# One attention pipeline around the expert stage, and the value products ahead of the logits in a slot

## The chip, the cores and the metric

The kernel runs on one core of a Trainium2 chip. The time is that of one launch on the device, in microseconds (us). All arithmetic is float32, or float32r: a float32 rounded so that TensorE takes it in one pass, and a product that must be exact is three such passes over a high and a low part.

## The reference, cut to what matters

```python
x  = L0_attn_X                      # 32 sequences x 256 rows x 128
xn = layernorm(x)
# attention: 16 heads of 64; position bias from 10 basis functions per head
Q, K, V = xn@Wq + bq, xn@Wk, xn@Wv
R = xn@Wr + br                      # 10 numbers per head and row
logits = Q K^T / 8 + causal mask + sum_n R[t, n] * b_nd[n, t - p]   (0 <= t - p < 128)
A = softmax(logits) V @ Wproj + bproj
# mixture of 8 experts, 128 -> 512 -> 128, two per row, weights softmaxed
top, idx = top_k(xn @ router_w.T, 2)
F = sum_k softmax(top)[k] * (gelu(xn w1[idx_k] + b1) w2[idx_k] + b2)
out = x + A + F
```

## The kernel before, in words

Every engine runs one list of instructions in order, written out by hand; semaphores tie the lists together. After a preparation (norm, weights split into two parts, router and the place of every row) come three stages.

**Attention of sequences 0 to 15.** A sequence has four quads of heads (a quad is two pairs, a pair two heads), and each engine takes one *slot* per quad (`sequence`, TensorE's at L1494). A slot `d` of TensorE holds, in this order: `keys` (L1430, queries and keys of the next quad's first pair), a *unit* at place 0, `logits` of quad d (L1450), `values` of quad d-2 (L1463, probabilities times values), units at place 1, `turn_probs` (L1439, transposed probabilities of quad d-1, first pair), `keys` of the next quad's second pair, units at place 2, `outputs` of quad d-2 (L1483, projection), units at place 3, `turn_probs` of the second pair. A unit is a product for the values ("v"), for R ("r", of the next sequence) or for the position bias ("g"); the table `UNITS` (L355) says in which slot and place it stands and whether it belongs to the next sequence. All units use one PSUM bank, so each waits until ScalarE has copied the one before (`unit_taken`). A "g" unit ("g", half t) reads `rT`, which SyncE fills by six transfers in `spread_weights` (L499) from the rounded R; its result goes to `gst`, by DMA to `skew` in HBM and back into `extra`, shifted along the diagonal.

ScalarE's slot (L852) is: copy of the value unit, copy of the first keys into `qk` (it waits until the logits that read that half of `qk` are done), exponentials of quad d's first pair, first tile (`exponentials`, two of 128x128, L839), copy of `headT` (`heads_out`, L845: what `values` made), copy of the unit at place 1, exponentials of the first pair's second tile, unit at place 2, second keys, unit at place 3, four exponentials of the second pair.

VectorE's slot (L1161) is: inverses; `bias_sums` of the first pair (L1136: it merges the two halves of the logits, adds the bias and takes the minimum, L1143 and L1149); `copy_probs` (L1125); `bias_sums` of the second pair; `copy_probs`; `add_heads` of quad d-2 (L1184, L1191), which frees the bank that `values` and `outputs` share; in the third stage `add_rows` adds the experts' rows. `values` waits for `add_heads` of the quad before. GpSimd scales the probabilities (`norms`) and moves rows by indirect DMA.

**Experts.** The rows of each expert lie in 39 blocks of 512. TensorE's `experts` (L1386) transposes block b+1 (`turn_x`), makes block b's hidden layer and block b-1's output. Before this stage the attention pipeline is emptied: two more slots hold values, transposes and outputs of sequence 15 alone. On four engines the middle of the stage is a loop.

**Attention of sequences 16 to 31** starts from nothing: SyncE spreads R of sequence 16, the first five "g" units follow each other, then slot 0. At the end the pipeline is emptied again.

The tiles of the experts and of attention overlap in SBUF.

## Time and profile before

| | |
|---|---|
| median of 3 runs | 1521.05 us (1520.63 to 1524.2) |
| the profiled execution, whole | 1505.93 us |
| its span, first to last instruction | 1503.8 us |
| TensorE busy (matmul) | 1341.1 us, 89% |
| ScalarE busy | 996.9 us, 66% |
| VectorE busy | 836.5 us, 56% |
| GpSimd busy | 765.9 us, 51% |
| mean granted TensorE clock | 0.959 |

The profile is of one execution, whose whole time is 15.1 us below the median. A row of a timeline gives its start in us from the span's beginning, its length, engine, source line, operation, what it writes and reads, and in brackets how long the engine was idle before it and what ended that. Matmuls overlap: the time that one takes on the engine is the distance to the next start. Two attention stages of about 525 and 535 us stand around an expert stage of about 266 us.

### The profile page before, as it was taken

What the parts mean: (1) busy time and instruction counts of PE and PEld (TensorE: products, weight loads), DVE (VectorE), ACT (ScalarE), POOL (GpSimd) and SP (SyncE); (2) the same over time, 40 slices, a digit from 0 to 9 for tenths busy, and PEclk for the clock granted to TensorE, in tenths of its full rate; (3) what the DMA queues carried; (4) which work ended last, traced back from release to release, by engine and by line L of the source; (5) the groups of instructions that cost most, each with busy time, mean ns of one, the idle gap of its engine ahead of it and who ended that gap; (6) DMA issues with size and microseconds to landing.
All of it is one profiled execution on the core that took longest, in us unless ns stands there. A gap on an engine that the chain in (4) does not pass through costs nothing.

```text
span 1503.8 us, 36197 instructions
## 1 busy us (share of the span) xinstructions
PE 1341.1 (89%) x10631; PEld 1118.1 (74%) x10631; DVE 836.5 (56%) x3523; ACT 996.9 (66%) x3088; POOL 765.9 (51%) x1518
## 2 busy tenths in 40 slices
PE   2472899999999999989999999599999999999997
PEld 1131688788878788868999999477887877778885
DVE  4675466666666666662222121156676666667766
ACT  1131688788888788865454544277888877788885
POOL 0340567777766777760000000177776666777764
PEclk8795899999999999999999999699999999999999
DMA  9775577777777677755666665476776777777773
GB/s 288 265 245 194 159 206 211 196 208 202 201 198 217 197 210 201 201 169 161 206 199 204 200 205 183 119 195 195 205 215 194 198 193 195 203 203 212 196 201 92
DMA packets 458681, 298.62 MB, mean 199 GB/s; under 512 B 20586, under 2 KB 432788, under 8 KB 458516
## 3 DMA queue, kind: packets, MB, share of 16 engines
q1 hardware_dynamic: 450324, 279.86, 64.4%
q0 software_dynamic: 8192, 16.79, 3.9%
q8 instruction: 75, 1.23, 0.3%
q14 instruction: 90, 0.74, 0.2%
HBM read 135.01 MB, written 145.77 MB: 187 GB/s over the span
## 4 chain that ended last, share of the span: by engine, by line
PE 69%; SPq 13%; DMA 8%; DVE 3%; issue 3%; ACT 2%; POOL 1%; DVEq 0%; POOLq 0%; ACTq 0%
PE ps L1459 10%; PE ps L1382 9%; PE ps L1478 9%; SPq L507 8%; PE ps L1346 8%; PE ps L1348 7%; PE ps L1347 7%; PE ps L1446 6%; PE ps L1488 5%; PE ps L1415 5%; DMA rT<-r_lo 5%; DMA skew<-gst 2%; ACT gst L814 1%; PE ps L1364 1%; SPq L482 1%
## 5 line engine op out<-in xcount | busy, mean ns | idle before, releaser
L839 ACT ACTIVATE prob<-logit,low 128x128 f32<-128x128 f32 x1024 | 402.1, 398 | 19.2 <-DVE low L1149 5.6
L1149 DVE CUSTOM_DVE_ANT_0 logit<-ps,extra 128x128 f32<-128x128 f32 x1024 | 256.1, 288 | 125.7 <-PE ps L1459 116.5
L1131 DVE TENSOR_TENSOR probT<-ps,keep 128x512 f32<-128x512 f32 x256 | 177.1, 692 | 240.0 <-PE ps L1446 240.0
L713 POOL TENSOR_SCALAR prob<-prob,inv 128x128 f32<-128x128 f32 x512 | 186.7, 365 | 153.2 <-DVE inv L1159 151.8
L669 POOL CAST r_hi<-r_raw 80x512 fp32r<-80x512 f32 x32 | 19.4, 607 | 411.3 <-ACT r_raw L808 411.3
L814 ACT COPY gst<-ps 128x512 f32<-128x512 f32 x256 | 150.9, 590 | 114.0 <-PE ps L1415 102.2
L1459 PEld LDWEIGHTS ps<-qk 64*128 64x128 f32 x2048 | 169.7, 190 | 61.3 <-issue 48.9
L1459 PE MATMUL ps<-qk 64*128 64x256 f32 (+1 forms) x2048 | 206.7, 342 | 0.0
L1478 PE MATMUL ps<-probT,val 128*64 128x256 f32 (+1 forms) x2048 | 194.7, 332 | 7.0 <-DVE acc L1191 7.0
L839 ACT ACTIVATION_READ_ACCUMULATOR prob<-logit,low 128x1 f32 x1024 | 196.5, 192 | 0.0
L1415 PE MATMUL ps<-basis,rT 120*128 120x512 f32 x256 | 129.2, 505 | 69.1 <-DMA rT<-r_lo 59.8
L715 POOL TENSOR_SCALAR prob<-prob,inv 128x128 f32<-128x128 f32 x512 | 185.5, 362 | 0.0
L1478 PEld LDWEIGHTS ps<-probT,val 128*64 128x64 f32 x2048 | 127.4, 136 | 59.2 <-issue 4.3
L829 ACT COPY qk<-ps 128x512 f32<-128x512 f32 x256 | 149.4, 583 | 32.2 <-PE ps L1459 26.1
L1346 PE MATMUL ps<-xq_hi,wqk_hi 128*128 128x256 f32 x512 | 167.0, 326 | 2.7 <-ACT qk L829 2.7
L1446 PE MATMUL ps<-ident,prob 128*128 128x128 f32 x1024 | 154.7, 273 | 4.3 <-POOL prob L715 3.6
L681 POOL DMA_INDIRECT x_place<-xrow,at_now x128 | 129.0, 1008 | 41.9 <-issue 28.3
L1382 PEld LDWEIGHTS ps<-w2b,hid 128*128 128x128 f32 x1248 | 145.2, 192 | 3.3
L1348 PE MATMUL ps<-xq_hi,wqk_lo 128*128 128x256 f32 x512 | 146.6, 286 | 0.0
L1347 PE MATMUL ps<-xq_lo,wqk_hi 128*128 128x256 f32 x512 | 146.2, 286 | 0.0
L1382 PE MATMUL ps<-w2b,hid 128*128 128x128 f32 x1248 | 145.4, 275 | 0.0
L683 POOL DMA_INDIRECT yget<-y_place,at_now x128 | 128.3, 1003 | 31.7 <-issue 27.3
(176 smaller groups left out, 2475.6 us busy)
## 6 DMA issues: line engine op xcount, KB each, us to landing
skew<-gst SPq DMA_DIRECT2D x384, 256.0 KB
extra<-skew SPq DMA_DIRECT2D x256, 256.0 KB, 3.8
w1b<-w_d SPq DMA_DIRECT2D x39, 514.0 KB, 3.6
w2b<-w_d SPq DMA_DIRECT2D x39, 320.0 KB, 3.4
rT<-r_hi SPq DMA_DIRECT2D x128, 80.0 KB
x_place<-zero SPq DMA_DIRECT2D x39, 256.0 KB, 2.8
placed<-x_place SPq DMA_DIRECT2D x39, 256.0 KB, 3.8
y_place<-yrow SPq DMA_DIRECT2D x39, 256.0 KB, 2.3
```

The source lines that it names most:

```text
L713: nc.gpsimd.tensor_scalar(prob[:, h, 0:P], prob[:, h, 0:P], inv[:, h, 0:1], 1.0, ALU.mult, ALU.mult).then_inc(norm_made, 1)
L715: nc.gpsimd.tensor_scalar(prob[:, h, P:], prob[:, h, P:], inv[:, h, 1:2], 1.0, ALU.mult, ALU.mult).then_inc(norm_made, 1)
L839: ins = nc.scalar.activation(prob[:, h % PB, cols], logit[:, h % LB, cols], ACT.Exp, scale=-1.0, bias=low[:, h % LB, t:t + 1], accum_out=t ...
L1149: ins = nc.vector.tensor_tensor_reduce(out=logit[:, h % LB, cols], in0=ps[:, b + n, cols], in1=extra[:, h, cols], scale=1.0, scalar=BIG, o ...
L1346: nc.tensor.matmul(dst, a_hi, b_hi, start=start, stop=False)
L1347: nc.tensor.matmul(dst, a_hi, b_lo, start=False, stop=False)
L1348: return nc.tensor.matmul(dst, a_lo, b_hi, start=False, stop=stop)
L1382: mm = nc.tensor.matmul(ps[:, Y_BANK[u], t * P:(t + 1) * P], hid[:, u, c, t * P:(t + 1) * P], w2b[:, u, c * P:(c + 1) * P], start=(c == 0) ...
L1415: mm = nc.tensor.matmul(ps[:, MISC_BANK, :], rT[:, par, n // 2, n % 2, tile * P:(tile + 1) * P], basis[:, :], start=True, stop=True)
L1446: mm = nc.tensor.transpose(ps[:, PT_BANK, a:a + P], prob[:, (2 * pair + n) % PB, k * P:(k + 1) * P], ident[:, :])
L1459: mm = nc.tensor.matmul(ps[:, S_BANK[pair % 2][n], cols], qk[rows, pair % 2, 0, q], qk[rows, pair % 2, 1, k], start=True, stop=True)
L1478: mm = nc.tensor.matmul(ps[DQ * n:DQ * n + DQ, HEAD_BANK, q], val[:, s, v:v + DQ], probT[:, hh % 4, p], start=(s == 0), stop=(s == 1), ski ...
```

## The change

- TensorE: in a slot `values(i, d - 2)` stands ahead of `logits(i, d)`. No other engine's slot is reordered.
- `UNITS`: the next sequence's first "g" unit moves from the end of slot 1 to place 1 of slot 2, the second to place 3 of slot 2, the third and fourth to places 1 and 2 of slot 3. Slot 1 has one "g" unit fewer, slot 3 one more.
- One pipeline over all 32 sequences. The expert stage stands inside it, in front of slot 0 of sequence 16: values and outputs of quads 2 and 3 of sequence 15 come after the experts, and the "g" units and keys of sequence 16 before them. Each engine waits for what its half-done work needs.
- The experts' loops are written out. SyncE fetches the experts' first weights and rows during sequence 15.
- SyncE: a bias transfer back is issued after the next write or two of the same sequence, and no longer carried over to the next.
- SBUF is laid out anew so that what lives across the expert stage (`extra`, `val`, `probT`, `qk`, `prob` and others) does not overlap it; `rT` is two tiles.

The hunks are, in order: the table, SyncE's order, ScalarE's, VectorE's, TensorE's slot and TensorE's list.

```diff
-        UNITS = [(0, 0, "v", 0, 0, 0), (0, 1, "g", 2, 1, 0), (0, 2, "r", 0, 0, 1), (0, 3, "g", 3, 0, 0),
-                 (1, 0, "v", 0, 1, 0), (1, 1, "g", 3, 1, 0), (1, 3, "g", 0, 0, 1),
-                 (2, 0, "v", 1, 0, 0), (2, 1, "g", 0, 1, 1), (2, 3, "g", 1, 0, 1),
-                 (3, 0, "v", 1, 1, 0), (3, 1, "g", 1, 1, 1), (3, 3, "g", 2, 0, 1)]
+                 (1, 0, "v", 0, 1, 0), (1, 1, "g", 3, 1, 0),
+                 (2, 0, "v", 1, 0, 0), (2, 1, "g", 0, 0, 1), (2, 3, "g", 0, 1, 1),
+                 (3, 0, "v", 1, 1, 0), (3, 1, "g", 1, 0, 1), (3, 2, "g", 1, 1, 1), (3, 3, "g", 2, 0, 1)]
...
             def sequence(i, more=True):
-                positions(i, POSITIONS_OWN[:2])
+                write_unit(i, *POSITIONS_OWN[0])
+                write_unit(i, *POSITIONS_OWN[1])
+                read_unit(i, *POSITIONS_OWN[0])
                 if more:
                     spread_weights(i + 1)
+                read_unit(i, *POSITIONS_OWN[1])
+                positions(i, POSITIONS_OWN[2:])
                 if i >= HALF + 2:
                     store(i - HALF - 2)
-                positions(i, POSITIONS_OWN[2:])
                 if more:
-                    positions(i + 1, POSITIONS_AHEAD)
+                    positions(i + 1, POSITIONS_AHEAD[:2])
+                    if i == HALF - 1:
+                        first_rows()
+                    positions(i + 1, POSITIONS_AHEAD[2:])
...
+            for i in range(B):
+                if i == HALF:
+                    for t in range(2):
+                        act.wait_ge(skew_out[t], (HALF * GROUPS + 3 - t) * 16 * (t + 1))
                     high_part(0, 0)
-                    for b in range(3):
+                    for b in range(PLACES):
                         experts(b, b % 2, b // 2)
...
+            for i in range(B):
+                if i == HALF:
+                    dve.wait_ge(prob_made, HALF * PAIRS)
                     low_x(0, 0)
...
                     if heads:
                         units(i, d, 0, more)
-                        logits(i, d)
                     if here(i, d - 2, heads, start):
                         values(i, d - 2)
+                    if heads:
+                        logits(i, d)
...
+            for i in range(B):
+                if i == HALF:
+                    unit_taken(pe, *START[-1], HALF)
                     turn_x(0, 0, 0)
+                    pe.wait_ge(logit_made, HALF * PAIRS)
+                    pe.wait_ge(pT_made, HALF * PAIRS - 2)
+                    pe.wait_ge(key_made, HALF * PAIRS + 2)
+                    for b in range(PLACES):
                         experts(b, b % 2, b // 2, b % ROWS_AHEAD, b // ROWS_AHEAD)
                     expert_out(PLACES - 1, (PLACES - 1) % 2, (PLACES - 1) // 2)
+                    pe.wait_ge(y_made, PLACES)
+                sequence(i, 0, more=i + 1 < B)
+            sequence(B, 0, heads=False, more=False)
```

## Rows read from the trace of the kernel before

**Rows 1.** Waits of TensorE, 300 to 660 us: total us, times, longest
```profile
PE ps L1415 <- DMA rT<-r_lo: 13.2, 11, 1.6
```

**Rows 2.** Timeline of TensorE: start us, us, operation; one slot, and the next slot's logits
```profile
1028.40 1.58 PE L1459 MATMUL ps<-qk 64*128 64x256 f32 x16
...
1029.91 1.52 PE L1478 MATMUL ps<-probT,val 128*64 128x256 f32 x16
...
1031.36 0.50 PE L1415 MATMUL ps<-basis,rT 120*128 120x512 f32 x1
...
1032.84 1.05 PE L1488 MATMUL ps<-wproj,headT 128*128 128x128 f32 x8
...
1033.65 0.48 PE L1415 MATMUL ps<-basis,rT 120*128 120x512 f32 x1
...
1033.97 0.60 PE L1446 MATMUL ps<-ident,prob 128*128 128x128 f32 x4
...
1034.32 0.36 PE L1346 MATMUL ps<-xq_hi,wqk_hi 128*128 128x256 f32 x1
...
1035.12 0.39 PE L1346 MATMUL ps<-wv_hi,xq_hi 128*128 128x512 f32 x1
...
1035.92 1.58 PE L1459 MATMUL ps<-qk 64*128 64x256 f32 x16
```

**Rows 3.** Timeline of ScalarE in the same slot
```profile
1029.42 0.59 ACT L829 COPY qk<-ps 128x512 f32<-128x512 f32 x1 [0.18 <-PE ps L1459]
1030.39 0.40 ACT L839 ACTIVATE prob<-logit,low 128x128 f32<-128x128 f32 x1 [0.38 <-DVE low L1149]
1030.79 0.39 ACT L839 ACTIVATE prob<-logit,low 128x128 f32<-128x128 f32 x1
1031.47 0.59 ACT L849 COPY headT<-ps 128x512 f32<-128x512 f32 x1 [0.20 <-PE ps L1478]
1031.96 0.59 ACT L814 COPY gst<-ps 128x512 f32<-128x512 f32 x1
...
1033.22 0.58 ACT L829 COPY qk<-ps 128x512 f32<-128x512 f32 x1
```

**Rows 4.** Timeline, the emptying of the pipeline after sequence 15
```profile
672.34 0.63 PE L1446 MATMUL ps<-ident,prob 128*128 128x128 f32 x4
...
674.51 1.52 PE L1478 MATMUL ps<-probT,val 128*64 128x256 f32 x16 [1.54 <-DVE acc L1191]
676.07 0.59 ACT L849 COPY headT<-ps 128x512 f32<-128x512 f32 x1 [4.96 <-PE ps L1478]
676.71 1.16 PE L1488 MATMUL ps<-wproj,headT 128*128 128x128 f32 x8 [0.68 <-ACT headT L849]
```

**Rows 5.** Timeline of TensorE: logits of slots 0 and 1, a "g" unit
```profile
1003.82 1.58 PE L1459 MATMUL ps<-qk 64*128 64x256 f32 x16
...
1012.09 1.58 PE L1459 MATMUL ps<-qk 64*128 64x256 f32 x16
...
1018.62 0.47 PE L1415 MATMUL ps<-basis,rT 120*128 120x512 f32 x1 [1.03 <-DMA rT<-r_lo]
```

**Rows 6.** Timeline of TensorE: first and last logits of each attention stage, expert products
```profile
153.22 2.93 PE L1459 MATMUL ps<-qk 64*128 64x256 f32 x16
...
661.56 1.58 PE L1459 MATMUL ps<-qk 64*128 64x256 f32 x16
...
679.79 0.47 PE L1346 MATMUL ps<-xb_hi,w1b 128*128 128x512 f32 x1 [0.76 <-DVE xb_lo L1216]
...
936.65 7.30 PE L1382 MATMUL ps<-w2b,hid 128*128 128x128 f32 x64
...
969.47 2.93 PE L1459 MATMUL ps<-qk 64*128 64x256 f32 x16
...
1481.27 1.58 PE L1459 MATMUL ps<-qk 64*128 64x256 f32 x16
```

**Rows 7.** Windows: length, busy (instructions) by engine, TensorE clock, DMA share, GB/s
```profile
663.00:680.00 17.00, 11.86 (x101) 8.89 (x98) 8.57 (x32) 6.34 (x21) 7.05 (x19) 1.00 0.47 144
```

More of the change, by code:

```diff
@@ L482, in read_unit @@
                 sp.dma_start(dst, src).then_inc(skew_in[2 * g + t], 16)
-            written = []
             def positions(i, units):
-                for g, t in units:
-                    wait_from(sp, skew_in[2 * g + t], i * 16)
+                for n, (g, t) in enumerate(units):
                     write_unit(i, g, t)
-                    if written:
-                        read_unit(*written.pop())
-                    written.append((i, g, t))
-            def positions_end():
-                read_unit(*written.pop())
+                    if n > 0:
+                        read_unit(i, *units[n - 1])
+                read_unit(i, *units[-1])
             def spread_weights(seq):
@@ L544, in _ @@
             fetch_rows(0)
-            for i in range(HALF):
-                sequence(i, i + 1 < HALF)
             def first_weights(b, u, k):
@@ L583, in experts, with first_rows @@
                     block_out(b - 1, 1 - u, None)
-            sp.wait_ge(logit_made, HALF * PAIRS)
-            first_weights(0, 0, 0)
-            second_weights(0, 0, 0)
-            sp.wait_ge(spread, TILES * TOP * 16)
-            for b in range(3):
-                block_rows(b, b)
-            for b in range(BLOCKS_FIRST):
-                experts(b, b % 2, b % ROWS_AHEAD)
-            with sp.Fori(0, BLOCK_TURNS) as m:
-                for r in range(ROWS_AHEAD):
-                    b, u, _ = block_of(m, r)
-                    experts(b, u, (BLOCKS_FIRST + r) % ROWS_AHEAD)
-            for b in range(BLOCKS_FIRST + ROWS_AHEAD * BLOCK_TURNS, PLACES):
+            def first_rows():
+                first_weights(0, 0, 0)
+                second_weights(0, 0, 0)
+                sp.wait_ge(spread, TILES * TOP * 16)
+                for b in range(3):
+                    block_rows(b, b)
+            for i in range(HALF):
+                sequence(i)
+            for b in range(PLACES):
                 experts(b, b % 2, b % ROWS_AHEAD)
             block_out(PLACES - 1, (PLACES - 1) % 2, None)
-            spread_weights(HALF)
-            positions(HALF, POSITIONS_AHEAD)
             for i in range(HALF, B):
@@ L705, in moves_of @@
             def moves_of(i, way, d, more):
-                moves = MOVES_FINAL if way is FORTH and not more else MOVES
+                moves = MOVES_FINAL if i == HALF - 1 else MOVES
                 return [n for n, at_d in enumerate(moves) if at_d == d]
@@ L741, in _ @@
             pool.wait_ge(xnT_made, 1)
-            for s0, way in ((0, FORTH), (HALF, BACK)):
-                s1 = s0 + HALF
-                if way is BACK:
-                    pool.wait_ge(s_psum, HALF * PAIRS)
-                split_q(s0, 0)
-                round_weights(s0)
-                if way is FORTH:
-                    pool.wait_ge(w_stored, 32)
-                    pool.wait_ge(zeroed, PLACES * 16)
-                    pool.wait_ge(route, 2)
-                sequence(s0, 0, way, s0)
-                for i in range(s0 + 1, s1 - 1):
-                    sequence(i, i % 2, way, s0)
-                sequence(s1 - 1, 1, way, s0, more=False)
-                sequence(s1, 0, way, s0, heads=False, more=False)
+            split_q(0, 0)
+            round_weights(0)
+            pool.wait_ge(w_stored, 32)
+            pool.wait_ge(zeroed, PLACES * 16)
+            pool.wait_ge(route, 2)
+            for i in range(B):
+                sequence(i, i % 2, FORTH if i < HALF else BACK, 0, more=i + 1 < B)
+            sequence(B, 0, BACK, 0, heads=False, more=False)
         @block.scalar
@@ L894, in high_part @@
                 nc.scalar.copy(xb_hi[:, u, :], ps[:, XB_BANK[u], :]).then_inc(xb_high, 1)
[L896 to L907 removed]
+            for n, (kind, k, t) in enumerate(START):
+                unit(n, kind, k, t, 0)
+            keys(0, 0)
+            keys(0, 1)
+            for i in range(B):
+                if i == HALF:
+                    for t in range(2):
+                        act.wait_ge(skew_out[t], (HALF * GROUPS + 3 - t) * 16 * (t + 1))
                     high_part(0, 0)
[L909 removed]
+                    for b in range(PLACES):
                         experts(b, b % 2, b // 2)
[L911 to L915 removed]
+                sequence(i, 0, more=i + 1 < B)
+            sequence(B, 0, heads=False, more=False)
         @block.vector
@@ L1232, in experts @@
                     block_y(b - 1, 1 - u, k if u == 1 else k - 1)
[L1234 to L1248 removed]
+            for i in range(B):
+                if i == HALF:
+                    dve.wait_ge(prob_made, HALF * PAIRS)
+                    low_x(0, 0)
+                    for b in range(PLACES):
                         experts(b, b % 2, b // 2)
                     block_y(PLACES - 1, (PLACES - 1) % 2, (PLACES - 1) // 2)
+                sequence(i, 0, more=i + 1 < B)
+            sequence(B, 0, heads=False, more=False)
             for d in range(2 * TOP):
```

132 lines of the change are left out of this document (37 added, 95 removed).

## The prediction

> **What bounds the kernel now.** First the table of engines: TensorE is busy 89% of the span and no other engine above 66%. Then TensorE's waits in the middle of the first attention stage: in 360 us it waited for one thing worth naming, the landing of `rT`, 13.2 us in 11 times [rows 1], one per sequence. Then one slot in the timeline: from logits at 1028.40 to the next logits at 1035.92 the starts follow each other without a gap, so a slot of two "g" units is 7.52 us of pure TensorE work [rows 2]. ScalarE in the same slot has small waits (0.18, 0.38, 0.20) and stays ahead [rows 3]. A sequence is 1035.92 - 1003.82 = 32.10 us: slot 0 (with the "r" unit) 8.27, slots 2 and 3 7.52 each, which leaves 8.79 for slot 1, 1.03 of it the wait for `rT` [rows 2, 5]. Last, the ends of the stages: between the last logits of sequence 15 and the first of 16 lie 307.9 us, of which the expert products hold 943.95 - 679.79 = 264.2 [rows 6]; emptying and filling cost the other 43.7.
>
> **The wait for `rT` goes.** The first "g" unit that reads the new `rT` stood at the end of slot 1, and stands after place 0 of slot 2 now. It was 1.03 us too early [rows 5] and comes some 4 us later, so nothing is late in its place. Slot 1 also loses one unit, 0.32 us (1033.65 to 1033.97, [rows 2]), and slot 3 gains it. If nothing else changed, the slots would be 8.27, 7.2, 7.52 and 7.84: 30.85 per sequence.
>
> **One pipeline.** TensorE enters the experts after the second transposes of slot 3. Behind it ScalarE still has its last exponentials and the wait for `skew` writes, queued ahead of the first cast of expert rows, and VectorE the subtraction behind that. I take 5 us from transposes to first product (at least 2, if only the cast and the subtraction are left; at most 8, if the last write's landing shows in full). Then 264.2 of expert products, unchanged (weights and rows were fetched ahead there too), and 1.9, an estimate (at least 1, at most 4), for the last block's result, which TensorE now waits for before it goes on, and for ScalarE's change back to the exponential in slot 0. Insertion: 271 us, in place of 307.9 less one slot.
>
> **Values ahead of logits.** This is the part that decides. Let S be the start of `values` in a slot. Values take 1.45 (1029.91 to 1031.36), so the logits start at S+1.45, and the unit at place 1 at S+2.95 as before; from there TensorE's list is the old one and reaches the outputs at S+4.44 (1032.84 - 1028.40) [rows 2]. ScalarE's order is unchanged, and everything in it from the copy of `qk` on hangs on the logits. Before, the first exponential started 1.99 after the logits (1030.39 - 1028.40), released by VectorE, whose list is likewise bound to them; `headT`, behind two exponentials, could start 0.79 later (0.40, 0.39) but waited for the values until 3.07 [rows 3]. Now: first exponential S+1.45+1.99 = S+3.44, `headT` S+4.23 to 4.82, and the outputs, 0.05 behind its end (676.66 to 676.71, [rows 4]), S+4.87 in place of 4.44. ScalarE goes on: the unit's copy at S+4.72 (0.49 behind), two exponentials, second `qk` at S+5.98 (1.26 behind), done at 6.56 [rows 3]. TensorE: outputs 0.81, unit 0.32, transposes 0.35, so keys could start at S+6.35, but their bank is free at S+6.61. Keys and the value unit take 1.60 (1034.32 to 1035.92, [rows 2]): the next S is at S+8.21, not 7.52.
>
> A second chain comes to nearly the same point. `values` waits for `add_heads` of the quad before, which stands behind both `copy_probs`; emptying the pipeline shows it alone: transposes 672.34, values 674.51, 2.17 later [rows 4]. TensorE's own way is 1.95 (1033.97 to 1035.92), and the logits used to hide the rest. This alone costs 0.22 per slot, and in slots where ScalarE binds it is covered.
>
> Slot by slot. Slot 2: 8.21. Slot 1: one unit less, but `qk` binds: 8.2. Slot 3, three units: the one at place 2 waits for the copy of the first (S+4.72+0.59+0.05 = 5.36, where TensorE is at S+4.44); then unit 0.32, outputs 0.81, the third unit waits for the second's copy, which takes the place of `qk` at S+5.98, until 6.62; unit, transposes, keys and value unit 0.32+0.35+1.60 give 8.9, the second chain 6.94+2.17 = 9.1, the write of `gst` that must have landed about as much: 9.2. Slot 0: the same with the "r" unit, 0.4 longer: transposes at S+7.24, plus 2.17 = 9.4. A sequence: 9.4+8.2+8.2+9.2 = 35.0 us, 4.15 above 30.85. Its bounds: 31.7 if only the second chain costs (four times 0.22), 36.5 if each slot also loses the 0.38 that ScalarE spends waiting for VectorE [rows 3]. I take the schedule, 35.0, since every step of it is a row of the same slot.
>
> **The sum,** first logits (153.22) to last (1481.27), 1328.05 us before [rows 6]. After: sequence 0, whose first slots have no values, 33.7 (7.9+8.4+8.2+9.2); 30 x 35.0 = 1050; insertion 271; sequence 31 up to its last slot, three slots of 8.2, 24.6. Together 1379.3, +51.3; the last logits stand 1.45 later in their slot; what lies before and behind is as it was. 1505.93 + 52.7 = 1558.7 us for the profiled execution. The median of the runs is 15.1 above it, which I add: **1574 us**. Put as gains and losses: some 80 us won by the wait, the restart and smoother sequences, 133 us (32 x 4.15) lost by the new order.
>
> **At no cost.** The written-out loops: the expert products ran with no gap between blocks in the loop, and the attention stages are written out already. SyncE's last reads now wait for their write to land, but no unit is due in those 2 to 3 us; if it were, that wait would come back once per sequence. SyncE's first expert transfers stand in slot 3 of sequence 15 once, beside 4 us in which no write is due. GpSimd has its inverses 0.5 into the slot as before and 2.5 us of room; if the cover went, the transposes would wait.
>
> **A rule that speaks against the change.** With ScalarE's waits TensorE would be busy some 88% of a slot and idle in pieces of 0.2 to 0.9 us. While the pipeline emptied it was busy 11.86 of 17 us, with longer gaps, and the granted clock was 1.00, its 2.4 GHz level [rows 7]. The Trainium skill, "TensorE: Matmul & The Clock Gate" (A second HAM failure mode: psum-queue depth-cycling), says that short idle pieces between groups of matmuls can make the clock oscillate between its two levels; by that rule the time would be the last rival's.
>
> **Rivals.**
> 1. Faster: ScalarE's chain does not bind. Its place is the start of `headT`, its price 4.15 less 0.88 per sequence. For it: ScalarE has idle time in each slot. Against: that idle time is all ahead of `headT`, and the list is in order. Then a sequence is 31.7 and the sum 33+30 x 31.7+271+23.2 = 1278, -50: 1472 us. It decides from a mean slot 0.44 us shorter than mine: at a sequence of 33.2 us the gains and losses meet. 10%.
> 2. In between: a sequence of 33.2, no change, 1521 us. Both chains half covered. 4%.
> 3. The change does not do what it says, in that a wait per sequence remains or comes anew on SyncE's or ScalarE's side (a landing of a write, 1 us each): 36.0 per sequence, 1604 us. 8%.
> 4. Slower still: the clock falls. At the lower level the logits of a slot took 2.93 in place of 1.58 [rows 2, 6]; one slot in ten at 1.9 times its length adds 12.8 x 7 = 90 us: 1660 us. 4%.
>
> **Numbers.** My forecast has 74%, its own range 1555 to 1595 (0.6 us per sequence either way). Below it lie rival 1 and 2 (14%), above it 3 and 4. The range 1540 to 1606 leaves out rival 1, 2 and 4. About 0.3% either way is what this kernel's measurement can tell. Slower 74+8+4 = 86%, less 1 for tails: 0.85; faster 0.12; same 0.03.
>
> **What would show it.** In the profile after: slots of 8.2, 8.2, 9.2 and 9.4 us between starts of values; a wait of TensorE's outputs for ScalarE's `headT` in every slot, 0.4 us; no wait for `rT` in mid-stage; ScalarE's wait for the values before `headT` gone and its wait for the logits before `qk` grown to about 1.4 us; about 271 us added between slot 3 of sequence 15 and slot 0 of 16. I am wrong if the slots stay at 7.5 to 7.7 us, or if TensorE's waits are for VectorE alone.

## The result, and the profile after the change

| | before | after |
|---|---|---|
| median of the runs, us | 1520.84 (1515.09 to 1524.2, 4 runs) | 1607.38 (1604.31 to 1611.28, 4 runs) |
| ratio to before | | 1.0575, 95% interval 1.0534 to 1.0615 |
| profiled execution, us | 1505.93, span 1503.8 | 1611.28, span 1609.5 |
| mean granted TensorE clock | 0.959 | 0.961 |
| first logits to last logits, us | 1328.05 | 1434.87 |

The change made the kernel 5.75% slower. The forecast was 1574 us with a range to 1606: the direction held, the time lies 33 us above the forecast and 1.4 us above the range. The first view is the page's table of engines, after, with the row of TensorE's clock in 40 slices.

```profile
PE 1401.6 (87%) x10631; PEld 1145.8 (71%) x10631; DVE 831.2 (52%) x3523; ACT 979.5 (61%) x3088; POOL 767.2 (48%) x1518
...
PEclk7795999999999999999999999999999999999999
```

TensorE issues as many instructions as before, and its mean clock is the same. Most of the time went into waits. The next view is TensorE's waits in the middle of the first attention stage (300 to 660 us) and then in the second (1035 to 1560 us): total us, times, longest.

```profile
PE ps L1296 <- ACT gst L783: 11.1, 20, 0.8
PE ps L1365 <- ACT gst L783: 3.4, 7, 0.7
...
PE ps L1428 <- DVE acc L1149: 1.1, 2, 0.7
```

```profile
PE ps L1428 <- DVE acc L1149: 35.0, 23, 2.2
PE ps L1365 <- ACT gst L783: 6.6, 14, 0.7
PE ps L1296 <- ACT gst L783: 6.2, 14, 0.5
```

The wait for `rT` of [rows 1] is gone from the middle of the stage. In its place stand waits for ScalarE's copies of units (`gst`), in both stages, and in the second stage alone a large one: the values wait for the additions on VectorE, 35.0 us, up to 2.2 us at a time. A wait names only who came last. The next two timelines show that in both stages part of it begins on TensorE itself, with a signal that comes late.

In its first part a slot of the first half is what the prediction drew up. The timeline of slot 2 of sequence 13, all engines (start, length, operation, idle time before it and who ended it):

```profile
629.15 1.58 PE L1409 MATMUL ps<-qk 64*128 64x256 f32 x16
630.18 0.59 ACT L798 COPY qk<-ps 128x512 f32<-128x512 f32 x1 [1.08 <-PE ps L1409]
630.88 0.40 ACT L808 ACTIVATE prob<-logit,low 128x128 f32<-128x128 f32 x1
...
631.66 0.56 ACT L818 COPY headT<-ps 128x512 f32<-128x512 f32 x1
...
632.28 1.16 PE L1438 MATMUL ps<-wproj,headT 128*128 128x128 f32 x8
...
633.19 0.48 PE L1365 MATMUL ps<-basis,rT 120*128 120x512 f32 x1
...
634.96 0.59 ACT L783 COPY gst<-ps 128x512 f32<-128x512 f32 x1 [1.00 <-PE ps L1365]
...
635.60 0.50 PE L1296 MATMUL ps<-wv_hi,xq_hi 128*128 128x512 f32 x1 [0.61 <-ACT gst L783]
...
637.97 1.58 PE L1409 MATMUL ps<-qk 64*128 64x256 f32 x16
```

In [rows 3] ScalarE waited 0.20 us for the values before `headT`, and 0.18 for the logits before `qk`. Now `headT` finds its values done, and `qk` waits 1.08. The first exponential stands 1.73 us behind the logits, where [rows 3] had 1.99, so `headT` holds the outputs up only a little: they start 0.06 us behind its end. What the prediction did not have comes next. The "g" unit that starts at 633.19 takes 0.48, but ScalarE, idle for 1.00 us, copies it only at 634.96, and the value unit behind that copy starts 0.61 late. The rest of this section shows the same delay at greater length in the second half, and what it goes with.

A slot of the second half looks different. The same view for slot 1 of sequence 17, with GpSimd's indirect moves:

```profile
1044.49 1.58 PE L1409 MATMUL ps<-qk 64*128 64x256 f32 x16
...
1047.08 1.03 POOL L660 DMA_INDIRECT yget<-y_place,at_now  x1 [0.16 <-issue]
...
1048.41 0.95 POOL L660 DMA_INDIRECT yget<-y_place,at_now  x1 [0.30 <-issue]
1048.61 0.60 PE L1396 MATMUL ps<-ident,prob 128*128 128x128 f32 x4
...
1049.67 0.94 POOL L660 DMA_INDIRECT yget<-y_place,at_now  x1 [0.30 <-issue]
...
1051.67 0.69 DVE L1093 TENSOR_TENSOR probT<-ps,keep 128x512 f32<-128x512 f32 x1 [2.37 <-remote]
...
1052.61 0.41 DVE L1149 TENSOR_TENSOR acc<-ps,acc 128x256 f32<-128x256 f32 x1
1053.16 1.87 PE L1428 MATMUL ps<-probT,val 128*64 128x256 f32 x16 [2.15 <-DVE acc L1149]
```

The transposes start at 1048.61 and take 0.60; the copy that waits for them starts at 1051.67. The profile can't name who released it and writes "remote". The records of the semaphores say why: TensorE's increments for the outputs, the transposes, the keys and the value unit, whose modelled ends are 1048.77, 1049.21, 1050.32 and 1051.01, all appear between 1051.55 and 1051.77. In the kernel before, the increments of TensorE in the middle of the attention stages stand within 0.03 us of the instruction's modelled end. After, some records are also missing (117 for 128 outputs, 215 for 256 keys), so the counts below are rough.

Here I call an increment late when its record stands more than 0.5 us behind. Each record is set against the last instruction of its semaphore that had ended, so of two that come in one burst on one semaphore only one is counted. That matters where logits stand first: counted one to one, slot 2 of the first half has 58 for the 44 given below (e1), 60 for 45 (f1), 68 for 54 (f4) and 57 for 40 (g2), and slots 2 and 3 of e1's second half 42 and 26 for 30 and 14. The other counts stay, but for a 13 in place of a 12 in g2. In the middle sequences (1 to 14 and 17 to 30) there are 0 late ones before and 156 after, all in slots 1 and 2, up to 2.8 us. The burst of sequence 13 above is one of them: the "g" unit's increment appears at 634.94, 1.27 us behind its modelled end, and those of the outputs and the transposes within 0.1 us of it. So late signals stand in slots 1 and 2 of both halves; in slot 1 of the first they cost nothing by the table below. Those of ScalarE and VectorE are not late in this kernel: nearly all their records stand within 0.02 us of the instruction's end.

The DMA engines show something at the same instant. Windows of 1 us, columns as in [rows 7]:

```profile
1048.00:1049.00 1.00, 1.00 (x11) 0.97 (x10) 0.97 (x6) 1.00 (x6) 0.70 (x2) 1.00 0.44 96
1049.00:1050.00 1.00, 0.87 (x7) 0.66 (x6) 0.30 (x4) 1.00 (x6) 0.69 (x2) 1.00 0.96 60
1050.00:1051.00 1.00, 1.00 (x6) 0.54 (x4) 0.00 (x0) 0.84 (x5) 0.61 (x1) 1.00 0.81 242
1051.00:1052.00 1.00, 0.01 (x1) 0.00 (x0) 0.33 (x1) 0.21 (x1) 0.00 (x0) 1.00 1.15 346
```

From 1049 to 1050 the DMA engines are taken 0.96 of the time and move only 60 GB/s; two us later they move 346.

TensorE's clock shows it too. The next windows are the slot above from its logits to the end of the wait, and the 3.2 us behind it:

```profile
1044.50:1054.20 9.70, 7.42 (x62) 6.14 (x62) 5.55 (x26) 5.81 (x21) 5.79 (x12) 1.00 0.61 160
1054.30:1057.50 3.20, 3.20 (x22) 2.48 (x18) 0.62 (x5) 0.67 (x2) 3.05 (x8) 0.50 0.32 85
```

Behind the 2.15 us without work the granted clock stands at 0.50, its 1.2 GHz level, for some 3.4 us, and the next logits take 2.85 us for 1.58. This happens in 7 of the 14 sequences 17 to 30, each time behind an idle stretch of 1.9 to 2.2 us in slot 1; but six sequences with as long a stretch keep 1.00. The seven take 38.17 us on average, the six 37.31. In the first half the clock stays at 1.00 throughout.

Means of a slot, from logits to logits, by the timeline of TensorE (first half: sequences 1 to 13, second half: 17 to 29), with the number of late increments by slot:

| kernel | first half: slots 0, 1, 2, 3, sum | second half: slots 0, 1, 2, 3, sum | last logits of 15 to first of 16 | late, first half / second half (slots 0 to 3) |
|---|---|---|---|---|
| before | 8.27 8.92 7.52 7.52, 32.24 | 8.27 9.22 7.63 7.52, 32.64 | 307.9 | none / none |
| forecast | 9.4 8.2 8.2 9.2, 35.0 | the same | 280 | |
| after | 9.14 8.20 8.87 9.05, 35.25 | 9.14 10.42 9.30 8.83, 37.69 | 287.1 | 0 33 40 0 / 0 51 32 0 |

Last, the way into the experts and out of them:

```profile
709.30 1.58 PE L1409 MATMUL ps<-qk 64*128 64x256 f32 x16
...
712.65 1.53 SPq L551 DMA_DIRECT2D placed<-x_place  x3
...
714.29 2.75 SPq L461 DMA_DIRECT2D skew<-gst  x2
...
720.17 0.59 ACT L783 COPY gst<-ps 128x512 f32<-128x512 f32 x1 [5.58 <-DMA skew<-gst]
...
720.81 1.97 PE L1314 MATMUL ps<-ident,placed 128*128 128x128 f32 x8 [5.71 <-ACT gst L783]
...
724.41 1.07 ACT L863 CAST xb_hi<-ps 128x512 fp32r<-128x512 f32 x2 [2.11 <-DMA skew<-gst]
...
725.94 0.76 PE L1296 MATMUL ps<-xb_hi,w1b 128*128 128x512 f32 x1 [3.16 <-DVE xb_lo L1174]
```

```profile
719.80:729.80 10.00, 5.83 (x17) 4.68 (x18) 1.29 (x2) 5.35 (x14) 0.00 (x0) 0.50 0.77 205
```

The first expert product comes some 11 us after the last transposes, where I had taken 5. Behind these waits the granted clock is 0.50 from 719.7 to 729.9, where the kernel before entered the experts at 1.00 (680 to 690 us), and the expert products take 266.65 us for 264.2. At the exit TensorE waits 0.78 us for the last block's result, within the 1.9 that the forecast had for this and ScalarE's change back.

### The profile page after: what moved, and what is told of

Read it like the earlier page. It is cut to its first block, busy times and chain, and to the rows that moved or that the text cites. A ratio compares the mean times of both kernels' runs of the same rounds, so it can differ in the third digit from the quotient of the medians.

```text
span 1609.5 us, 35362 instructions
## 1 busy us (share of the span) xinstructions
PE 1401.6 (87%) x10631; PEld 1145.8 (71%) x10631; DVE 831.2 (52%) x3523; ACT 979.5 (61%) x3088; POOL 767.2 (48%) x1518
## 4 chain that ended last, share of the span: by engine, by line
PE 66%; DVE 9%; issue 8%; ACT 6%; DMA 3%; SPq 3%; another core or an unknown queue 2%; POOL 1%; DVEq 1%; ACTq 0%; POOLq 0%
PE ps L1428 12%; PE ps L1409 9%; PE ps L1332 9%; PE ps L1296 7%; PE ps L1298 6%; PE ps L1297 6%; PE ps L1438 6%; PE ps L1396 5%; PE ps L1365 5%; DVE logit L1111 3%; ACT gst L783 3%; ACT prob L808 3%; DMA skew<-gst 2%; DVE probT L1095 1%
## 5 line engine op out<-in xcount | busy, mean ns | idle before, releaser
L1428 PE MATMUL ps<-probT,val 128*64 128x256 f32 (+1 forms) x2048 | 200.3, 338 | 52.7 <-DVE acc L1149 46.0
L1428 PEld LDWEIGHTS ps<-probT,val 128*64 128x64 f32 x2048 | 142.5, 139 | 130.5 <-ACT val L771 38.4
L1409 PE MATMUL ps<-qk 64*128 64x256 f32 (+1 forms) x2048 | 210.9, 347 | 0.0
L1409 PEld LDWEIGHTS ps<-qk 64*128 64x128 f32 x2048 | 172.9, 194 | 37.2 <-issue 23.9
L1438 PE MATMUL ps<-wproj,headT 128*128 128x128 f32 x1024 | 141.3, 281 | 3.0 <-ACT headT L818 2.3
L1396 PEld LDWEIGHTS ps<-ident,prob 128*128 128x128 f32 x1024 | 126.2, 140 | 23.6 <-POOL prob L692 6.1
```

What stands on the lines that cost most here:

```text
L1396: mm = nc.tensor.transpose(ps[:, PT_BANK, a:a + P], prob[:, (2 * pair + n) % PB, k * P:(k + 1) * P], ident[:, :])
L1409: mm = nc.tensor.matmul(ps[:, S_BANK[pair % 2][n], cols], qk[rows, pair % 2, 0, q], qk[rows, pair % 2, 1, k], start=True, stop=True)
L1428: mm = nc.tensor.matmul(ps[DQ * n:DQ * n + DQ, HEAD_BANK, q], val[:, s, v:v + DQ], probT[:, hh % 4, p], start=(s == 0), stop=(s == 1), ski ...
L1438: mm = nc.tensor.matmul(ps[:, HEAD_BANK, t * E:(t + 1) * E], headT[:, pair, t * P:(t + 1) * P], wproj[:, (2 * quad + pair) % PAIRS, :], st ...
```

## The experiments

The kernel before ran again beside each group of experiments (medians 1522.93 beside e1 to e4, 1518.09 beside f1 to f4, 1521.49 beside g1 to g3), and each ratio is to it. Each experiment is named by its label, e1 to g3. Of the theories that the expectations number, the third is that three or more indirect moves of GpSimd in a row make TensorE's completion signals late; the fourth, that SyncE's reads standing ahead of its own writes do it.

### e1: the order put back in the changed kernel

```
                     units(i, d, 0, more)
+                    logits(i, d)
                 if here(i, d - 2, heads, start):
                     values(i, d - 2)
-                if heads:
-                    logits(i, d)
```

> The change with the slot's order on TensorE undone: logits ahead of values, all else kept. Theory 1 (the new order costs, the rest gains): slots back to 8.3, 7.2, 7.5 and 7.9 us, a sequence 30.9 to 31.2 in both stages, about 1435 us (1425 to 1455). Theory 2 (what made sequences 16 to 31 cost 2.4 us more than 0 to 15 lies in the new SyncE order or unit table and is independent of the order on TensorE): slots 1 and 2 of the second stage stay 0.5 to 2 us above those of the first, 1470 to 1500 us.

Measured: 1484.17 us (1480.92 to 1485.64; a single further run took 3048.71 and stands out of the comparison), ratio 0.9745 [0.9693, 0.9798]. Slots 8.27 7.27 7.68 8.36, 31.57, and 8.27 7.27 8.41 8.83, 32.77; 288.35 between the halves; late 0 17 44 13 / 0 26 30 14. The order alone costs 1607.38 - 1484.17 = 123 us; all the rest of the change gains 38.8. The forecast had 133 and 80. The time lies in the range of theory 2 and not of theory 1, though of theory 2's signs only one came: slot 2 is 0.73 longer in the second half, slot 1 is 7.27 in both. So the costs beside the order are larger than theory 1 had them. Slots 0 and 1 are as drawn up for the old order (8.27 and 7.2), slots 2 and 3 aren't (7.52 and 7.84). In the second half (1000 to 1400 us), ScalarE's waits of this kernel:

```profile
ACT val L771 <- remote: 14.3, 8, 1.8
ACT gst L783 <- DMA skew<-gst: 14.1, 12, 1.8
```

### e2: the new order alone, in the kernel before

The same four lines the other way round in the kernel before.

> The kernel before with one edit: values ahead of logits in TensorE's slot. Theory 1: the two chains behind the new order make slots of 8.2 to 9.4 us here too, while the wait for rT is covered by them: about 35 us per sequence in the first stage, and 37 in the second if what is late there comes with the order; 1610 to 1670 us. Theory 2: 35 us in both stages, about 1605 us, and no late signals of TensorE in slot 1.

Measured: 1614.73 us (1612.21 to 1620.21), ratio 1.0618 [1.057, 1.0666]. Slots 9.14 9.16 9.22 7.97, 35.49, and 9.14 9.97 9.33 7.97, 36.41; 306.95 between the halves; late 0 11 47 0 / 0 17 42 0. So the order costs 1614.73 - 1522.93 = 92 us there, in the range of theory 1. The late increments come with the order alone, without one pipeline: the instruction mix and the moves' order on GpSimd are those of the kernel before, which has none. The order is not needed for them either: e1 has the old one, and 144. Slot 3, with two units, is 7.97, near the 8.2 of the forecast's schedule; with three it is 9.05.

### e3: the moves spread in the changed kernel

```
-        MOVES = (1, 1, 1, 2, 2, 2, 3, 3)
+        MOVES = (0, 0, 1, 1, 2, 2, 3, 3)
```

> The change with GpSimd's eight indirect row moves of a sequence spread as two per slot, in place of none, three, three and two. Theory 3 (TensorE's completions are signalled late in slots 1 and 2 because three indirect moves stand there in a row): slot 1 of the second stage falls from 10.1 to 8.2 us or so and slot 2 in both stages from 8.8 or 9.3 towards 8.2, 25 to 50 us in all, 1555 to 1582 us. Rival (they are late for SyncE's transfers, or moves in slot 0 hurt as much): 1600 to 1620 us.

Measured: 1568.91 us (1561.97 to 1570.33), ratio 1.0295 [1.0247, 1.0343]. Second half 9.14 8.14 7.97 8.89, 34.15: slots 1 and 2 fell from 10.42 and 9.30 to the 8.2 of the forecast, and late increments from 83 to 26. First half 9.14 10.19 7.96 8.88, 36.16: there the transposes of slot 1 wait for the probabilities (26.1 us in 14 times) that GpSimd scales behind the moves, and the moves in slot 0 wait for rows that are fetched only then; in 7 of the 14 sequences the clock falls to its lower level behind that. The values' wait for the additions in the same sequences of the second half is 1.0 us in 3 times, where the changed kernel had 35.0 in 23. The third theory has its first support, and most of the miss is here: 3.54 us a sequence, of which some 0.4 is the clock, which stays at 1.00 in this second half.

### e4: SyncE's write ahead of its reads, in the changed kernel

```
+                write_unit(i, *POSITIONS_OWN[2])
                 read_unit(i, *POSITIONS_OWN[1])
-                positions(i, POSITIONS_OWN[2:])
+                read_unit(i, *POSITIONS_OWN[2])
```

> The change with SyncE's order after the six rT transfers as in the kernel before: the last own unit is written first, then the two transfers back. Theory 4 (the late signals in slot 1 come from a transfer back and the writes issued close behind it): slot 1 of the second stage falls towards 8.2 us, up to 30 us in all, 1575 to 1590 us. Rival: 1600 to 1615 us.

Measured: 1603.76 us (1603.53 to 1607.79), ratio 1.0546 [1.0502, 1.0589]. 35.07 and 37.41 a sequence, late 0 30 41 0 / 0 50 34 0. The fourth theory falls.

### f1: e1 with other moves and the weights fetched earlier

```
+        MOVES_BACK = (0, 0, 1, 1, 2, 2, 3, 3)      # sequences 16 to 31
...
+                if i == HALF - 1:
+                    first_weights(0, 0, 0)
+                    second_weights(0, 0, 0)
                 if more:
                     positions(i + 1, POSITIONS_AHEAD[:2])
```

with the order of e1.

> The changed kernel with three edits: the logits stand ahead of the value products in each slot again (as in e1), in sequences 16 to 31 the eight indirect moves stand as pairs (two in each slot) where they were three in slots 1 and 2, and the first expert's weights are fetched ahead of the last positions before the experts, so that the write of the skewed copy due then isn't behind them. Theory 3 (three indirect moves in a row make TensorE's completion signals late, 1 to 2.8 us in slots 1 and 2): the second half falls from e1's 32.77 us a sequence to about 31.3, 15 times, so 22 to 24 us less; theory of the entry (the write waits behind the weight issues on SyncE): the entry falls from 11 us towards 5, so 5 to 8 us less. Together about 1452 us (1440 to 1465). Rival (the late signals bind only where the value products stand first, and the entry is held by the transfer itself): as e1, 1478 to 1486.

Measured: 1473.23 us (1471.89 to 1476.68), ratio 0.9705 [0.9679, 0.9732], 11 less than e1 and 21 above the expectation. Both parts missed. The stretch between the halves is 288.18, as before the edit: the weights were not what held the write back (the rows' three transfers stood between still). And the second half is 8.66 7.27 7.58 8.73, 32.24: slot 2 gained 0.83, but slot 0 lost 0.39, and 20 late increments turned up in slot 0, where no kernel so far had one. The list offers an explanation: the first move of a slot stands ahead of the normalizing on GpSimd and the others behind it, so two in slot 0 and the first of slot 1 follow each other with only the rounding of R between them, two instructions. I had called them pairs. But e3 has the same list in slot 0 and no late increment there.

### f2: the heads drained earlier on ScalarE

```
                 units(d, 0)
+                if here(i, d - 2, heads, start):
+                    heads_out(i, d - 2)
                 if to_come:
                     keys(*later)
                 if heads:
                     exponentials(i, 2 * d, 0)
-                if here(i, d - 2, heads, start):
-                    heads_out(i, d - 2)
```

in the changed kernel (values first).

> The changed kernel with one move on ScalarE: the heads' outputs are drained ahead of the first copy of the keys and the first exponentials of the slot, not behind them. The theory of chain A (logits, exponentials on ScalarE, the copy of the heads, the outputs on TensorE, about 2 us between logits and outputs that nothing fills) says that slots 0 and 3 shorten by 0.3 to 1.0 each, and the other chain (the additions on VectorE that the value products wait for) takes over: 33.5 to 34.5 us a sequence in the first half in place of 35.2, in all 1555 to 1585. If the chain through the additions already sets every slot, the time stays at 1600 to 1610. If the later exponentials delay the transposes by more than the heads gain: above 1615.

Measured: 1589.58 us (1586.61 to 1594.3), ratio 1.0459 [1.0431, 1.0486]; 5 us above the expectation. Slots 8.66 8.25 8.99 8.62, 34.51, and 8.66 11.32 8.95 8.68, 37.62; late 0 37 54 0 / 0 54 50 0. ScalarE's chain is worth 0.48 us in slot 0, as drawn up, and in slot 3 0.43 in the first half and 0.15 in the second, but slot 1 of the second half loses more than was won. The increments are up to 3.1 us late there, TensorE's idle stretch is 2.3 to 2.8 us, where the changed kernel had mostly 2.0 to 2.2, and behind it the clock falls to its lower level for 3.4 us in all 14 sequences, where it did so in 7.

### f3: f2 with the additions earlier on VectorE

```
+                if here(i, d - 2, heads, start):
+                    add_heads(i, d - 2)
                 if here(i, d - 1, heads, start):
                     copy_probs(i, 2 * (d - 1) + 1)
-                if here(i, d - 2, heads, start):
-                    add_heads(i, d - 2)
```

> f2, and on VectorE the additions stand ahead of the second copy of the transposed exponentials. Both chains of the prediction are shortened. If the two chains are what lengthens a slot with the value products at its head, the slots fall towards the 7.5 to 8.3 of the old order: 32 to 33 us a sequence, in all 1490 to 1540. If VectorE's sum is what counts, the second copy is only late in its turn and the outputs wait for it: 1570 to 1610.

Measured: 1561.22 us (1557.23 to 1568.24), ratio 1.0291 [1.0251, 1.0332]: between the two expectations. Slots 8.47 7.74 8.98 8.49, 33.67, and 8.46 9.56 8.91 8.67, 35.6. Slot 0 has come down to 0.2 of the old order's 8.27. TensorE's waits in the second half (1040 to 1500 us) now name another partner:

```profile
PE ps L1428 <- DVE probT L1095: 15.7, 14, 2.5
```

The values wait for the copy of the second transposes, which is late because the increment of those transposes is: late 0 32 44 0 / 0 46 50 0.

### f4: f1 with the units dealt out evenly

```
-                 (3, 0, "v", 1, 1, 0), (3, 1, "g", 1, 0, 1), (3, 2, "g", 1, 1, 1), (3, 3, "g", 2, 0, 1)]
+                 (3, 0, "v", 1, 1, 0), (3, 1, "g", 1, 0, 1), (3, 3, "g", 1, 1, 1)]
```

and the units of slots 0 to 2 dealt out to match, so that slots 1 to 3 have two "g" units and slot 0 two and the "r" unit; all else as in f1.

> f1 with the units of the fetched keys dealt out so that each slot has two or three short ones and none has the third that waits for the write of the skewed copy to land (slot 3 had three). If that wait (about 1.1 us on TensorE in slot 3 of the changed kernel and of e1) is on the path, 31 sequences lose 0.5 to 1.1 each against f1: 15 to 30 us less, about 1430 to 1440. If the work only moves to another slot, within 5 of f1; if a unit then comes before its read has landed, slower than f1 by 10 or more.

Measured: 1449.89 us (1448.95 to 1451.84), ratio 0.9543 [0.9521, 0.9566], 23 less than f1. The difference is in the expected 15 to 30; the time is 10 above the range that was given with it, since f1 itself came out 21 higher. Slots 8.26 7.52 7.97 7.75, 31.51, and 8.44 7.68 7.71 7.52, 31.35; 283.27 between the halves. In the second half the gain is 0.89 us a sequence (15 of them: 13 us), in the first it is nearly nothing, 0.05: slot 3 is 0.54 shorter, slot 1 has the unit now (7.27 to 7.52), and slot 2 rose from 7.73 to 7.97 with 54 late increments in place of 45. Another 5 us come from the entry to the experts, where in the kernels with three units the third one's copy waits for a write to land (5.58 us in the view above). TensorE's wait for ScalarE's copies in the second half (1000 to 1400 us) is down to one, where e1 had 7.1 us in 11 times:

```profile
PE ps L1298 <- ACT gst L785: 1.1, 1, 1.1
```

### g2: the moves in a row at another place

e1 with

```
+        MOVES_BACK = (0, 0, 0, 1, 2, 3, 3, 3)      # sequences 16 to 31
```

which makes three in a row at the end of slot 0 and, behind the rounding of R, the first of slot 1 as a fourth; none in a row in slots 1 and 2, two in slot 3.

> e1 (logits ahead of the value products) with the eight moves of sequences 16 to 31 as four in a row behind slot 0, one and one, and two at the end. Theory 3 (moves in a row make completion signals late wherever they stand): in the second half slot 0 rises from 8.27 us to 8.8 or more and slot 2 falls from 8.41 to 7.5 or 7.6; the sum about as e1, 32.3 to 33.3 a sequence. Rival (the late signals belong to what else moves in slots 1 and 2, SyncE's writes and reads of the positions): slot 0 stays 8.27 and slot 2 stays above 8.2, or both are clean.

Measured: 1477.47 us (1473.35 to 1480.07), ratio 0.9702 [0.9671, 0.9733]. Second half 8.70 7.74 7.52 8.59, 32.54; late 0 15 40 12 / 45 0 0 6. This is the cleanest answer of the study. The late increments went with the moves: 45 in slot 0, where there were none, and none in slots 1 and 2, where there were 56; slot 0 rose from 8.27 to 8.70 (the theory had 8.8 or more) and slot 2 fell from 8.41 to 7.52, as the third theory said. (Slot 1 rose by 0.47, since the fourth move stands ahead of the normalizing that the transposes wait for.) SyncE's transfers kept their order, with those of slots 1 and 2 still there, so they alone do not make the signals late. In the timeline, slot 0 of sequence 21:

```profile
1113.07 0.95 POOL L661 DMA_INDIRECT yget<-y_place,at_now  x1 [0.30 <-issue]
...
1113.88 0.60 PE L1397 MATMUL ps<-ident,prob 128*128 128x128 f32 x4
...
1114.33 0.95 POOL L661 DMA_INDIRECT yget<-y_place,at_now  x1 [0.30 <-issue]
...
1115.38 0.69 DVE L1094 TENSOR_TENSOR probT<-ps,keep 128x512 f32<-128x512 f32 x1 [1.58 <-PE ps L1397]
```

The transposes' time to the copy is 1.50 us from start to start; in the same kernel three us earlier, with no move beside it, it is 0.64 (1110.84 to 1111.48).

### g1: values first with everything mended

f3 with the units and the weights of f4, and

```
+        MOVES = (1, 1, 2, 2, 3, 3, 3, 3)           # sequences 0 to 15
+        MOVES_BACK = (0, 1, 1, 2, 2, 3, 3, 3)      # sequences 16 to 31
```

so that at most two moves stand in a row, but for three at the end of slot 3 in the first half.

> The value products stay at the head of a slot, and everything that the runs so far name as a cost beside them is mended: heads and additions early (f3), no third unit in slot 3 (f4), and the eight indirect moves so that no more than two stand between two blocks of other work on GpSimd (three in the last slot of sequences 0 to 15). If late completion signals and the unit were what kept f3 above the old order, its 33.7 and 35.6 us a sequence fall to 31.5 to 32.3 and the kernel to 1450 to 1480. If the order itself keeps a price (each slot's value products wait for what VectorE finished last), it stays 1 us a sequence or more above f4, 1490 to 1530.

Measured: 1495.31 us (1493.06 to 1497.52), ratio 0.9833 [0.9802, 0.9864]. Slots 8.47 7.76 7.82 8.94, 32.98, and 8.47 8.27 8.06 7.90, 32.70. It comes out above the first expectation and inside the second: values first keeps a price of 1.6 us a sequence, 49 us in all, against g3, which differs from it only in the order on TensorE, ScalarE and VectorE. Not everything is mended, though: late 0 21 21 38 / 0 39 25 15, 159 in all and up to 2.0 us, where g3 has 91. How much of the 1.6 is theirs no run here tells.

### g3: f4 with the moves in pairs

The two lines of moves of g1, in f4 (logits first).

> f4 with pairs of moves: in f4 three still stood in a row in slots 1 and 2 of sequences 0 to 15 and in slot 0 of 16 to 31 (two there and the first of slot 1 behind them), and there its slots were 7.97 for 7.5 (slot 2) and 8.44 for 8.27 (slot 0). Theory 3: the first half falls from 31.5 to about 31.0 us a sequence, the second from 31.35 to about 31.1, so some 10 us less than f4, 1437 to 1445. Rival (two in a row are no better than three once nothing else is tight): 1447 to 1453.

Measured: 1445.99 us (1444.74 to 1448.51), ratio 0.9505 [0.948, 0.953]. Slots 8.39 7.52 7.91 7.57, 31.39, and 8.26 7.65 7.61 7.60, 31.12. It is 4 us less than f4 by the medians and not the 10 expected: the ranges of the two do not overlap, but each ratio's interval touches the other's. In the second half slot 0 behaves as the third theory said (8.44 to 8.26); in the first half slot 2 stays at 7.91 and slot 0 rises to 8.39 (f4: 7.97 and 8.26). The time lies between the two expectations. Late increments 10 15 17 23 / 0 17 3 6, shorter than before (in the first half at most 0.9 in slots 1 and 2, where they had been up to 2.5), and in slot 3, where three moves stand in a row now, up to 1.9. Pairs make signals late too, by less. This is the fastest version of the study: 5% faster than the kernel before. Its table of engines begins:

```profile
PE 1335.5 (92%) x10631; PEld 1115.5 (77%) x10631; DVE 837.3 (58%) x3523; ACT 988.3 (68%) x3088; POOL 764.5 (53%) x1518
```

## Why the prediction was right and where it was wrong

**The wait for `rT` goes: right.** It is gone from the middle of the stage, and nothing is late in its place. Slot 1 of e1 is 7.27, forecast 7.2.

**"If nothing else changed … 30.85 per sequence": wrong.** The forecast's time is not added up from it, but its account of gains and losses is. e1 is that case: 31.57 in the first half and 32.77 in the second. Slots 0 and 1 are right. Slot 3 is 8.36 and 8.83 for 7.84: its third unit waits for a write to land. I saw that landing in slot 3 of the new order and put it on a par with the chains; for the old order I left it out, and under "At no cost" wrote that no unit is due while a write lands. Slot 2 is 7.68 and 8.41 for 7.52, through late signals. Instead of "some 80 us won", the rest of the change won 39.

**Values ahead of logits: the chains are real, the size is partly luck.** The forecast had a cost of 133 us for this part; measured were 123 in the changed kernel and 92 in the kernel before. In the first half a sequence is 35.25, forecast 35.0. Within it the parts moved: slot 0 is 9.14 (9.4), since the exponential starts 1.73 behind the logits and not 1.99, and slot 2 is 8.87 (8.2), since signals are late there. That the sum still fits is luck: a term that the prediction did not have fills what its chains overstate. Putting `heads_out` early took 0.48 off slot 0, and the additions early another 0.19. The outputs' wait of 0.4 us for `headT` in every slot, named as a sign, came in slots 1 and 2 alone and as 0.13: there the outputs start 0.05 behind `headT`'s end in 52 of 56 slots, and 0.25 behind the matmul before them, where the kernel before had 0.12. In slots 0 and 3 `headT` was early. The order by itself costs less than 4.15 us a sequence where the moves stand alike: the second halves of e3 (values first) and f1 (logits first) have the same list of moves, and are 34.15 and 32.24, 1.91 apart, where the changed kernel and e1 are 4.92 apart. So more than half of the order's cost in the second half goes with where the moves stand.

**The same 35.0 for both halves: wrong, and the step that failed.** It is the term "30 x 35.0" of the sum: every slot was drawn up from rows of one slot in which each signal came on time. The second half took 37.69. The 2.44 above the first half, over 15 sequences, is 37 us, more than the miss of the median, 33. In its place the runs show TensorE's signals 0.5 to 2.8 us late in slots 1 and 2, and the values waiting for them. Some 7 of the 37 us are the clock at its lower level behind these waits (8 times, 0.9 us each by the means above). Spreading the moves took back 3.54 a sequence (34.15). The trace of the kernel before showed nothing of it: its signals are on time in both halves. Rival 3 had the right form, a new wait per sequence at 1604 us, but named SyncE and ScalarE and not GpSimd's moves.

**Entry to the experts, "5 us": wrong.** It is 11, and the products behind it took 2.4 us more than 264.2, with the clock at its lower level for the first 4 us. I counted the cast and the subtraction behind the exponentials, and bounded the rest by "the last write's landing shows in full", 8. There are two landings in a row: the third unit's copy waits for one (5.58), and its own write and the cast's wait for that (2.11) follow. Without the third unit the stretch is 5 us shorter. "SyncE's first expert transfers stand beside 4 us in which no write is due" was wrong too: a write came at 714.29, behind the rows' transfers of 712.65; but fetching the weights earlier gained nothing, so what these transfers cost was not separated.

**The clock: the rival's price is refuted, the effect is not.** The Trainium skill's "TensorE: Matmul & The Clock Gate" (A second HAM failure mode: psum-queue depth-cycling) had spoken for a clock that oscillates. In the first half, with waits of up to 0.8 us in most slots and single ones up to 1.8, the granted clock stayed at 1.00: there the trace does not bear that out. In the second, where TensorE stood idle for about 2 us at a time, the clock did oscillate: it went to 0.50 and back in 8 of 15 sequences, at some 7 us where rival 4 had 90; the kernel before did so 3 times there. The mean over the span, 0.961 against 0.959, hides this, since the kernel before spent 23.9 us at the lower level between its stages (948.4 to 972.3) and the changed one 10.2.

**The sum.** By logits the miss is 1434.9 - 1379.3 = 55.6 us: second half 41 (15 times 2.75, sequences 16 to 30), the stretch with sequence 15 and the experts 8, the first half 3, sequence 0 2, sequence 31 1. The forecast for the profiled execution, 1558.7, missed by 53. The 15.1 us added for the distance to the median covered part of that by luck: after the change the profiled execution is 4 above the median, and not 15 below. Two small sums of the prediction do not close, at no consequence: 8.27, 7.2, 7.52 and 7.84 are 30.83, and slot 0's transposes, 0.4 behind S+6.94, would be at 7.34 and not 7.24.

**What stays open.** Why the kernel before has no late signals with the same moves in a row. The new order alone brings them up there (e2), and the rest of the change brings them up without it (e1, whose moves in slot 1 of sequence 20 start within 0.02 us of where the kernel before has them); that SyncE's transfers fall at other instants is one guess, and e4 tested only one order of them. The moves in a row go with the long delays (e3, g2) but are not enough, as the kernel before and slot 0 of e3 show. Nor is it shown whether the increment is late or the matmul's own last write: the Trainium skill's "Perfetto Trace Analysis" (Tensor Engine Instruction (MATMUL, LD_WEIGHTS)) says that the profiler reports an estimated end for TensorE and that the semaphore is pushed only once all bytes are acknowledged. The trace agrees with either: what it shows is that modelled ends and increments, 0.01 to 0.03 us apart in the kernel before, are up to 2.8 us apart in the changed kernel and 3.1 in f2. That it is no effect of the profiler on itself follows from the plain runs, which moved by as much (1604 to 1609 us, and 1562 to 1570 with the moves spread). Nor is it shown why the clock fell in 7 sequences and not in 6 others with the same idle time.

## What to carry to other kernels

An order that keeps an in-order engine fed is a chain through every other in-order engine: write down, for each, what stands between the product moved back and the copy that TensorE waits for. Here one statement moved by 1.45 us cost 92 to 123, and 49 with the chains shortened and fewer moves in a row. When a stage is joined or unrolled, also look for the unit that waits for a transfer to land: it costs a little in every turn and much at a seam. And where GpSimd issues several indirect moves in a row beside other transfers, look at the waits that the profile calls "remote", and spread the moves. Read the clock by stretches as well: its mean over the span did not move while it fell in half of the sequences.

## What the runs showed of the hardware

TensorE's completion signals can reach the other engines 0.5 to 3.1 us late in two or more slots of a sequence, several in one burst (four within 0.22 us in the slot shown), there behind a stretch in which the DMA engines are taken 0.96 of the time at 60 GB/s. This followed GpSimd's rows of indirect moves from slot to slot (56 late increments in slots 1 and 2 became 0, and 0 in slot 0 became 45). In a list of 8 moves per sequence of 32 to 38 us, the place of the moves alone was worth 38 us of 1607 (moves spread, values first) and 4 of 1450 (logits first, units balanced); that a late signal costs more where the engines' chains have less slack is my reading of this, not shown by itself. Behind single idle stretches of 1.9 to 2.8 us TensorE's granted clock fell from 1.00 to 0.50 for some 3.4 us, in 7 of 13 such stretches of the changed kernel's sequences 17 to 30 and in 14 of 14 of f2, at 0.9 us each in the former; with waits of up to 0.8 us in most slots it stayed at 1.00 from 205 to 690 us.
